# A wait for each pair's gathers on GpSimd, and the edge part ahead of the node sums on TensorE

## What is computed

```python
q, k, v = x @ Wq + bq, x @ Wk + bk, x @ Wv + bv      # by node, (N, 8, 16)
e = edge_attr_128 @ We                               # by edge
k_e, v_e = k[src] + e, v[src] + e                    # the gather
alpha = einsum('ehd,ehd->eh', q[dst], k_e) / sqrt(16)
a = exp(alpha - segment_max(alpha, dst)[dst])
z = segment_sum(a, dst)
out = segment_sum((a / z[dst])[:, :, None] * v_e, dst)
x_r = x @ Wskip + bskip
beta = sigmoid([out, x_r, out - x_r] @ Wbeta)
out = layernorm(beta * x_r + (1 - beta) * out) * ln_gamma + ln_beta
y = layernorm(x + x + relu(out))
```

## Time and profile before

| | us |
|---|---|
| median of 3 runs | 2126.05 |
| lowest and highest run | 2125.98, 2133.83 |
| span of the profiled execution | 2774.7 |
| first gather of the loop starts in it at | 78.9 |
| last gather of the loop starts in it at | 2674.6 |

### The profile page before, as it was taken

One profiled execution on the slowest core, in us unless ns is written; L12 is line 12 of the kernel. 1 busy time (PEld: TensorE's weight loads), 2 busy tenths in 40 slices (PEclk: granted clock), 3 DMA queues, 4 the chain that ended last, 5 costly groups with the idle time before them and its releaser, 6 DMA issues.

```text
span 2774.7 us, 45026 instructions
## 1 busy us (share of the span) xinstructions
PE 2009.6 (72%) x11492; PEld 1805.8 (65%) x11492; DVE 1801.8 (65%) x4040; ACT 1140.6 (41%) x3750; POOL 1497.6 (54%) x1591
## 2 busy tenths in 40 slices
PE   7478888888776577667766767757687777778775
PEld 5467777777666566566665767656576667667664
DVE  7465565566666566566665667657676676777764
ACT  0133333344343344344443444434454454454455
POOL 0555555555556555565555555555555555555531
PEclk9677777777777777777777777778788777777786
DMA  8556666666655555555554655555565555555541
GB/s 308 185 165 184 176 184 183 178 180 180 172 167 167 158 159 167 154 174 165 167 167 143 176 163 167 175 149 165 164 176 167 170 176 168 169 172 180 169 123 39
DMA packets 298585, 468.47 MB, mean 169 GB/s; under 512 B 49862, under 2 KB 193034, under 8 KB 298230
## 3 DMA queue, kind: packets, MB, share of 16 engines
q1 hardware_dynamic: 222680, 259.30, 31.3%
q0 software_dynamic: 75648, 206.24, 26.2%
HBM read 414.62 MB, written 50.73 MB: 168 GB/s over the span
## 4 chain that ended last, share of the span: by engine, by line
PE 54%; issue 17%; another core or an unknown queue 13%; ACT 8%; DVE 3%; DMA 2%; ACTq 1%; POOL 0%; SPq 0%; POOLq 0%; DVEq 0%
PE sum_ps L928 18%; PE q_ps L825 12%; PE e_ps L812 10%; ACT dist_en L1046 3%; PE max_ps L841 2%; PE sum_ps L866 2%; PE sum_ps L865 2%; PE sum_ps L851 2%; PE max_ps L834 2%; PE sum_ps L850 2%; ACT hot_en L1055 1%; PE sum_ps L894 1%; PE sum_ps L895 1%; DMA xt_buf<-xT 1%
## 5 line engine op out<-in xcount | busy, mean ns | idle before, releaser
L706 POOL DMA_INDIRECT kv<-kv_tab,src_all x1568 | 1483.1, 946 | 1144.6 <-DVE kve L1373 683.8
L1373 DVE TENSOR_TENSOR kve<-kv,e_ps 128x1024 f32<-128x1024 f32 x392 | 462.2, 1218 | 756.0 <-issue 626.2
L928 PE MATMUL sum_ps<-wv,hot_en 128*128 128x136 f32 x3136 | 683.7, 394 | 15.0 <-issue 11.4
L928 PEld LDWEIGHTS sum_ps<-wv,hot_en 128*128 128x128 f32 x3136 | 626.1, 291 | 60.4 <-issue 58.5
L825 PE MATMUL q_ps<-q_win,hot_ne 128*128 128x128 f32 x3136 | 458.8, 284 | 265.2 <-issue 262.8
L825 PEld LDWEIGHTS q_ps<-q_win,hot_ne 128*128 128x128 f32 x3136 | 401.5, 197 | 281.0 <-issue 278.1
L1046 ACT ACTIVATE dist_en<-iota_n,neg_rel 128x128 bf16<-128x128 f32 x1568 | 497.7, 389 | 75.9 <-issue 75.9
L812 PE MATMUL e_ps<-we,ea 128*128 128x128 f32 x3136 | 422.6, 292 | 13.1 <-issue 7.2
L1083 ACT COPY sums<-sum_ps 128x136 f32<-128x136 f32 x392 | 98.3, 263 | 798.5 <-remote 730.6
L812 PEld LDWEIGHTS e_ps<-we,ea 128*128 128x128 f32 x3136 | 415.3, 212 | 12.7 <-issue 6.4
L834 PE MATMUL max_ps<-ident,top 128*1 128x128 f32 x196 | 65.0, 332 | 332.8 <-ACT used_b L1060 296.5
(11 more groups left out here) (136 smaller groups left out, 1573.7 us busy)
## 6 DMA issues: line engine op xcount, KB each, us to landing
ea<-eaT SPq DMA_DIRECT2D x196, 512.0 KB
row_b<-rel_row SPq DMA_DIRECT2D x196, 256.0 KB
kv<-kv_tab,src_all POOLq DMA_INDIRECT x1568
q_win<-q_tab SPq DMA_DIRECT2D x392, 64.0 KB
sum_tab<-sums SPq DMA_DIRECT2D x392, 59.5 KB
kv_tab<-tab_buf SPq DMA_DIRECT2D x33, 384.0 KB, 3.7
logit<-sum_tab SPq DMA_DIRECT2D x49, 136.0 KB
xt_buf<-xT SPq DMA_DIRECT2D x33, 192.0 KB, 4.0
```

Source lines behind the costliest of these rows:

```text
L706: pool.indirect_dma_start(out=kv[:, s, t, :], out_offset=None, in_=kv_tab[:, :], in_offset=bass.IndirectOffsetOnAxis(ap=src_all[:, tile:ti ...
L928: mm = pe.matmul(sum_ps[u][:, 0:AC], hot_en[:, s, t, :], wv[:, s, t, :], start=(t == 0), stop=(t == TILES_G - 1))
L1373: dve.tensor_tensor(kve[:, s, :, :, :], kv[:, s, :, :].rearrange("p t (a c) -> p t a c", a=2), e4.to_broadcast([P, TILES_G, 2, C]), ALU.ad ...
```

## The change

GpSimd: before the first gather of pair q it waits until both slots of pair q - 1 have received all that pair's gathers. (The count for a slot is 16 for a tile, 4 tiles a pair, and every second pair uses the slot.) TensorE: in each step the edge part of the next pair is issued before the node sums of the last pair, not behind them. Nothing else changes; the same instructions are issued on all engines, and 390 waits more on GpSimd.

```diff
             def gather(q):
                 par = q % 2
+                if q:
+                    for u in range(2):
+                        pool.wait_ge(kv_ld[2 * (1 - par) + u], 16 * TILES_G * ((q - 1) // 2 + 1))
                 for u in range(2):
                     s = 2 * par + u
                     if q >= 2:
...
             def step(q, par, i, sums=True, first_use=False, last=False, top=True, spread=True):
+                if not last:
+                    for u in range(2):
+                        edge_part(q + 1, 1 - par, u, i + par, False)
                 if sums:
                     for u in range(2):
                         node_sums(q - 1, 1 - par, u, first_use)
-                if not last:
-                    for u in range(2):
-                        edge_part(q + 1, 1 - par, u, i + par, False)
                 if not last:
                     for u in range(2):
                         q_spread(q + 1, 1 - par, u, i + par, False)
```

## The result

The changed kernel takes **2753.18 us** (median of its runs, 2744.96 to 2760.87) where the kernel before takes 2126.02 us: ratio 1.292, 95% interval 1.2892 to 1.2948. The forecast was 2442 us, with a range up to 2560. It is slower, as forecast, but by 627 us and not by 316. A fourth run of the changed kernel took 5167.5 us at a mean TensorE clock of 0.339, where the other three had 0.757 to 0.759, and is not in these numbers.

What follows compares the result with a forecast made beforehand. The prediction took GpSimd's serial issue of gathers as the bound. The added wait, 1.62 us at 195 places, gave +316 us and TensorE's order 0, so 2126 + 316 = 2442 us, range 2300 to 2560.

Steps and rivals of the forecast that it cites:

- The bound: GpSimd's serial issue of gathers, 1.25 us each, 10.0 us a pair, sets the kernel's time.
- Rivals 1 and 2: GpSimd has slack: the wait is hidden, 2126 us (chance 0.08), or the earlier edge part pays, 2030 us (0.06).
- Rival 1: Gather issue takes 1.02 us or less in plain runs, hiding the wait: 2126 us, +-10; chance 0.08.
- Part 1, the landing: GpSimd's added wait: a pair's last gather lands 2.6 us after its start, ends 2.1 and 3.9.
- Part 1, the wake: GpSimd's added wait: 0.27 us from landing to the next gather's start, second wait met soon after the first.
- Part 2 at 0: TensorE's new order: sums up to 2.3 us later, hidden; earlier e_ps worth nothing; costed at 0.
- cover: TensorE's slack before the next pair's prod wants the spread: over 5 us, enough to hide the later sums.
- I take it to belong to the profiled execution: The 13.1 us pair cycle, with instructions held up during gathers, was taken as absent from the plain runs.
- The hold-up: Engines' own instructions are held up while gathers run and let go when the DMA engines fall quiet.
- Rival 3: TensorE drops to half clock, a pair takes 13 us or more: 2711 us; chance 0.06, shared with landings near 3.9 us.
- What was to be seen: Changed trace: gather 8 to next gather 1 at least 2.4 us, e_ps right behind kve, 946 ns unchanged.
- Wrong on the size if the landing is not 2.6 us: Stated sign of failure: the forecast's size rests on a 2.6 us landing of a pair's last gather.

Runs made afterwards that it cites:

- e2: Changed kernel without the added wait, so TensorE's new order alone: 2133.06 us, ratio 1.0016 to the kernel before.
- e4: Kernel before with a ninth gather in each pair, into a buffer nobody reads: 2376.27 us, ratio 1.1159 to the kernel before.
- e14: Changed kernel waiting for the second group only, third time: 2681.0 us beside 2780.64 for the kernel before, ratio 0.9641.
- e1: Changed kernel with TensorE's old order, so the added wait alone: 2829.77 us, ratio 1.3293 to the kernel before.
- e6: Changed kernel with SyncE's loads of edge features and row_b cut to one or two numbers from the third pair on: 2608.62 us, ratio 0.9389 to before.
- e7: Changed kernel with TensorE's old order and SyncE's edge-feature and row_b loads cut from the third pair on: 2603.22 us, ratio 0.9369 to the kernel before.
- e9: Changed kernel run again without edit: 2665.02 us beside 2775.28 for the kernel before, ratio 0.9623.
- e11: Same edit as e6 to the changed kernel (light SyncE loads), run again: 2644.84 us, ratio 0.9528 to the kernel before.
- e12: Same program as e7 (changed kernel, old order, light SyncE loads), run again: 2779.2 us, ratio 1.0027 to the kernel before.
- e13: Changed kernel run once more without edit: 2664.59 us beside 2780.64 for the kernel before, ratio 0.9586.
- e15: Same edit as e6 to the changed kernel (light SyncE loads), third time: 2607.46 us, ratio 0.9375 to the kernel before.
- e5: Changed kernel waiting for the second group only, first time: 2667.02 us beside 2779.53 for the kernel before, ratio 0.9597.
- e10: Changed kernel waiting for the second group only, second time: 2827.78 us beside 2775.28 for the kernel before, ratio 1.0127.
- e3: Changed kernel with TensorE's old order and both waits moved to the pair before the last one, already landed: 2128.51 us, ratio 1.0002 to before.
- e8: Kernel before without the last gather of each pair from the third pair on: 2483.89 us, ratio 0.8942 to the kernel before.

## Why the prediction was right or wrong

**The bound: right.** GpSimd issues a gather each 1.25 us and stops nowhere between pairs in the short kind (e2), and a ninth gather costs 1.26 us (e4). Rivals 1 and 2 fall with that. Rival 1 wanted 1.02 us or less an issue.

**Part 1, the landing: the term that was mis-sized, and the step that failed.** I took 2.6 us. It measures 3.57 in the mean, from gather 8 to the start of the `kve` that waits for it. A fifth of the error, 0.2 us, was in my own rows. The earlier trace rows bounded the last packet to 2.1 to 2.6 us, and 2.42 is right; but I used a value between the last packet and the start of `kve`, 2.84 us, as if the release were earlier. Where the other packets take under 0.4 us `kve` starts 2.78 us after gather 8 at the median, so what I called the latest is the quiet case. The other part, 0.77 us in the mean, goes with the other queues' packets. The prediction named the bound for them, 3.9 us from the earlier trace rows, but gave landings near it only a share in a chance of 0.06 and let its own range end at 3.2. The trace of before could mislead there: measured as above, 161 of 195 of its places had under 0.4 us of other packets. (3.57 - 2.6) x 195 = 190 us. This alone carries the forecast to 2631 us, out of its range.

**Part 1, the wake: mis-sized.** I took 0.27 us from a gather that waited once and carries that wait itself. In the changed kernel the wait that stops stands in an instruction of its own, and the wake is 0.70; with one added wait the gather carries it, and the wake is 0.24 (the floors 3.4 and 3.0). I had looked only at whether the second wait is met soon after the first, and not at which instruction holds it. 0.43 x 195 = 84 us. The number of instructions alone doesn't tell the two apart: before has 45026, the kernel with one wait (e14) 45220, the changed one 45221, so either has one more a pair. ("Perfetto Trace Analysis" of the Trainium skill, section "Identifying Dependency Chains", says that an instruction with waits on several engines may get EventSemaphore instructions in front of it that hold the additional waits. These counts agree, and so do the semaphores that the trace gives for each; the page says nothing of the price.)

**A term that was missing.** Fourteen times, every 13th pair, the second gather of a pair starts 3.0 us after the first, not 1.25. GpSimd's timeline in the changed kernel:

```profile
430.16 0.95 POOL L709 DMA_INDIRECT kv<-kv_tab,src_all  x1 [2.48 <-issue]
433.15 0.94 POOL L709 DMA_INDIRECT kv<-kv_tab,src_all  x1 [2.04 <-issue]
```

14 x 1.74 = 24 us. It comes each 104 gathers in all kernels with both added waits (changed, e1, e6, e7, e9, e11, e12, e13, e15), at 7, 9 and 10 of these 14 places with one (e5, e10, e14), and nowhere in e2, e3 and e4, which never stop, nor in before and e8. e3 has one instruction fewer than the changed kernel, 45220. What it is the traces don't say.

**The sum, mended:** 316 + 190 + 84 + 24 = 614 us. The spans of the changed kernel and of e3 differ by 2743.4 - 2130.8 = 612.6, the medians of changed and before by 627.

**Part 2 at 0: right alone, wrong beside the wait.** e2 measures +0.2%. I looked for what the order costs on TensorE and for cover, and the cover was there. What I left out is in my own sentence on SP's queue: the loads go out at another time. With the wait in place the order is worth -77 us, and I take it that this time decides how often they meet the last gather. It was luck for the forecast: the wait alone, for which it had +316 us, costs 701 (e1), and the order hid a part of that.

**"I take it to belong to the profiled execution": wrong.** The hold-up is of some sessions, and there the plain runs are as long as the profiled one. The inference from 2774.7 against 2126 was sound in that the plain runs shown can't have had it, but the cause was not the profiler: the profiled executions of the changed kernel and of e1 to e4 are as long as their plain runs. There the change goes the other way: 2665 us, 4% less. The prediction gave for that case a span between 2454 and 2775 us, and it is 2649.4 (e13). A way to read it, argued and not tested: in before, the next gather waits for a `kve` that is let go only when the gathers stop, 2.84 + 1.22 + 0.27 = 4.33 us; with the wait it starts 3.5 us after gather 8, while `kve` runs. That fits the counts above, 188 gathers waiting for `kve` in before and 2 in e13.

**Rival 3: half of it came.** TensorE's mean clock did fall. Against the short kind, to which the changed kernel belongs, it went from 0.90 to 0.92 (the plain runs of before beside e1) to 0.757 to 0.759; against the profiled execution of before, at 0.770, hardly. But that cost nothing, since the spread was done before it was wanted, by 0.23 us at the least.

**What was to be seen.** No gap was under 2.4 us (least 3.37), 946 ns did not change, and `e_ps` stands right behind `kve`: all as said. "Wrong on the size if the landing is not 2.6 us" is what happened. The page "DMA: Bandwidth & Descriptors" of the Trainium skill, section "Anatomy of one DMA — SWDGE (gpsimd) path", gave an estimated 2.30 us, which counts the completion in. It is near the end of the last packet alone (2.42), 0.5 us short of what the waiting engine sees with little other traffic and 1.3 us short of what it sees here on average.

## What to carry to other kernels

A wait for a transfer just issued costs its landing as the waiting engine sees it, wake and all, less the issue interval it replaces, at every place; take the landing from the start of the instruction that consumed the data, not from the last packet, and size it for the traffic that will be about at that time, not for the quiet moment at which the old trace happens to show one. Waits that are already met cost nothing here (e3). Of several in front of an instruction that really stops, look for the one that stops and for what holds it: the wake was 0.24 us where the gather did, and 0.70 where an instruction of its own did. And when the profiled execution is 31% longer than the plain ones, look for a second condition of the chip in plain runs before laying it on the profiler: a change can be 29% slower in one and 4% faster in the other.

## What the runs showed of the hardware that was not expected

- The same program takes 2126 to 2129 us or 2775 to 2804 us, by session, for all of its runs there. In the long kind other engines' instructions seem to stand while GpSimd issues gathers. Its cause is open. The chip's number doesn't decide it: the one numbered 12 gave 2128.66 and later 2780.64.
- In the long kind variants are also less repeatable between sessions than before is: 2667 and 2828 us for one wait, 2603 and 2779 for the wait with light loads, though the changed kernel gave 2665 twice. How often gathers wait for `kve` goes with it (94 times in the 2828 us, never in the 2603).
- A gather starts 0.24 us after the `kve` that waits for the same landing where it carries that wait itself, and 0.70 us after it where the wait stands in an instruction of its own. Two waits that are met cost nothing (e3, within 0.12%).
- A gather's last packet ends 2.42 us after its start with the DMA engines otherwise quiet, and at 3.2 to 3.7 us in the changed kernel where other queues' packets take 0.4 us and more of the 2.4 us behind it.
- Every 104 gathers of a kernel that stops for each landing, one gather is 1.74 us late.
